# Sort stage of a graph kernel: one flag layout instead of two, and a strided read by TensorE

## The reference

```python
edge_index = jnp.stack([src, dst])
x = x + _L0_gnn_ref(_layernorm(x, axis=-1), edge_index, edge_weight, W, a1, a2)
x = x + _L0_ffn_ref(_layernorm(x, axis=-1)[None], ...)[0]
# inside the graph layer:
support = x @ W
r_D = jax.nn.sigmoid(support @ a2)
gated = r_D * support
msg = gated[col] * edge_values[:, None]
out = jax.ops.segment_sum(msg, row, num_segments=n)
sumnorm = jax.ops.segment_sum(edge_values * r_D[col, 0], row, num_segments=n)
```

## Time and profile before

| | |
|---|---|
| time before, median of 3 | 1416.52 us (1414.48 to 1417.66) |
| profiled execution, its own time | 1417.25 us |
| its span | 1415.4 us |
| granted TensorE clock, mean | 0.934 |
| busy: PE, DVE, POOL, ACT | 1187.8, 1079.2, 912.0, 371.0 us |
| POOL's gathers in the sort, after it | 294, 516 |

### The profile page before, as it was taken

How to read it: one execution, slowest core, us unless ns; L and a number is a source line. 1 busy time by engine, 2 the same in 40 slices (tenths; PEclk the granted TensorE clock), 3 DMA queues, 4 the chain that set the end, 5 groups by cost and what they waited for, 6 DMA issues and landing times.

```text
span 1415.4 us, 21674 instructions
## 1 busy us (share of the span) xinstructions
PE 1187.8 (84%) x6271; PEld 922.5 (65%) x6271; DVE 1079.2 (76%) x2744; ACT 371.0 (26%) x1224; POOL 912.0 (64%) x895
## 2 busy tenths in 40 slices
PE   3788588778988889798988898878888888887998
PEld 2677577767877778594556655555565555556887
DVE  8888999999999999537777677776776778764322
ACT  0334111111100100002333343333333334333232
POOL 0289677777777777757777777777777777760000
PEclk9889889999999999859999999999999999999999
DMA  8112345575545455725644445644444444431021
GB/s 271 34 60 72 54 112 150 148 158 152 146 134 138 136 145 140 156 64 125 135 119 126 118 126 124 131 122 125 118 126 120 126 121 123 125 105 35 34 78 70
DMA packets 163415, 166.39 MB, mean 118 GB/s; under 512 B 84677, under 2 KB 135897, under 8 KB 163308
## 3 DMA queue, kind: packets, MB, share of 16 engines
q0 software_dynamic: 39712, 108.02, 29.0%
q1 hardware_dynamic: 102428, 37.71, 11.2%
q10 hardware_dynamic: 21168, 19.35, 4.5%
HBM read 136.86 MB, written 28.14 MB: 117 GB/s over the span
## 4 chain that ended last, share of the span: by engine, by line
PE 33%; DVE 25%; POOL 17%; issue 13%; DMA 8%; POOLq 2%; ACT 1%; SPq 0%; DVEq 0%; ACTq 0%
PE bank L1700 32%; POOL rows L830 17%; DMA rows<-gated_rows_dram,ring_i 7%; DVE big L964 5%; DVE big L934 5%; DVE S L1113 3%; DVE big L918 2%; POOLq L822 2%; DVE big L949 2%; DVE big L925 2%; DVE big L942 1%; PE bank L1764 1%; DVE big L1050 0%; DMA big<-in_edge_weight_dram 0%; DVE bank L956 0%
## 5 line engine op out<-in xcount | busy, mean ns | idle before, releaser
L1700 PE MATMUL bank<-rows,S 128*128 128x257 f32 (+1 forms) x2254 | 603.1, 398 | 97.6 <-DMA rows<-gated_rows_dram,ring_i 76.0
L830 POOL DMA_INDIRECT rows<-gated_rows_dram,ring_i x516 | 511.0, 990 | 170.4 <-issue 146.5
L1700 PEld LDWEIGHTS bank<-rows,S 128*128 128x128 f32 x2254 | 408.1, 194 | 248.4 <-DMA rows<-gated_rows_dram,ring_i 140.7
L737 POOL DMA_INDIRECT rows<-gated_rows_dram,lg x294 | 290.7, 989 | 106.7 <-issue 73.3
L1700 PE MATMUL bank<-big 128*104 128x128 f32 (+3 forms) x1824 | 227.6, 288 | 71.3 <-DVE big L964 71.3
L1700 PEld LDWEIGHTS bank<-big 128*104 128x104 f32 (+2 forms) x1824 | 223.5, 194 | 80.7 <-issue 77.9
L1287 DVE TENSOR_SCALAR S<-iota,lof,srec 128x128 f32<-128x128 f32 x588 | 167.0, 358 | 1.5 <-PE bank L1700 1.4
L1298 DVE TENSOR_TENSOR ag<-bank,ovr 128x257 f32<-128x257 f32 x49 | 20.9, 427 | 153.2 <-PE bank L1700 153.0
L1544 ACT COPY ovr<-bank 128x257 f32<-128x257 f32 x98 | 36.8, 375 | 322.4 <-PE bank L1700 302.6
L1700 PE MATMUL bank<-Wxs,xT 128*128 128x512 f32 x196 | 112.0, 700 | 0.1
L1700 PE MATMUL bank<-xn,lg 128*128 128x256 f32 x392 | 102.0, 385 | 0.0
(11 more groups left out here) (260 smaller groups left out, 1410.5 us busy)
## 6 DMA issues: line engine op xcount, KB each, us to landing
overflow_sums_dram<-ovr ACTq DMA_DIRECT2D x98, 128.5 KB
rows<-gated_rows_dram,ring_i POOLq DMA_INDIRECT x516, 2.9
gated_rows_dram<-rows SPq DMA_DIRECT2D x49, 128.5 KB, 2.3
ovr<-overflow_sums_dram SPq DMA_DIRECT2D x49, 128.5 KB, 2.5
rows<-gated_rows_dram SPq DMA_DIRECT2D x49, 128.5 KB, 2.2
out_dram<-S SPq DMA_DIRECT2D x48, 128.0 KB, 1.7
rows<-gated_rows_dram,lg POOLq DMA_INDIRECT x294, 3.1
res<-in_x_dram SPq DMA_DIRECT2D x1, 4352.0 KB
```

Of the source, the lines that this page charges most:

```text
L737: pool.indirect_dma_start(rows[:, turn(n), :], None, gtab[:, :], bass.IndirectOffsetOnAxis(ap=ring1[:, n:n + 1], axis=0)).then_inc(s_row[t ...
L830: pool.indirect_dma_start(rows[:, slot(b, u), :], None, gtab[:, :], bass.IndirectOffsetOnAxis(ap=ring_i[:, b // CH % 2, n:n + 1], axis=0)) ...
L1700: return nc.tensor.matmul(o, l, r, start=start, stop=stop, skip_group_check=True)
```

## The change

The flags with columns innermost (`flags4`) and the step `mark` that makes them are gone. `lookup` now multiplies `flagsj`, with buckets innermost, so `prod` lies with buckets innermost as well. `quads` reads it across: its moving operand steps over 52 elements of two bytes from one column to the next, and is cut at whole buckets; the products of `later` are read as before.

```diff
-        flags4 = halved(carve(NX * HC, BF16), HC)
...
-            def mark(g):
-                step(v.tensor_tensor(flags4, hib[:, g * GC:(g + 1) * GC].rearrange("p (h j) -> p h j", h=2).unsqueeze(1)
-                                     .broadcast_to([P, NX, 2, HC]),
-                                     numbers(g).unsqueeze(2).unsqueeze(3).broadcast_to([P, NX, 2, HC]), ALU.is_equal))
...
             def lookup(g):
                 dve.wait_ge(s_base, 2 * g + 2)
-                v.tensor_tensor(halved(prod[:, 0:NX * GC], HC), flags4,
-                                bank[0][:, 0:4 * NX].rearrange("p (h v b) -> p h v b", h=2, v=2)[:, :, 0, :].rearrange("p h b -> p b h").unsqueeze(3).broadcast_to([P, NX, 2, HC]),
+                v.tensor_tensor(prod[:, 0:NX * GC].rearrange("p (h j b) -> p h j b", h=2, b=NX), flagsj[g % 2],
+                                bank[0][:, 0:4 * NX].rearrange("p (h v b) -> p h v b", h=2, v=2)[:, :, 0:1, :].broadcast_to([P, 2, HC, NX]),
                                 ALU.mult).then_inc(s_prod, 1)
...
-            mark(0)
             lookup(0)
-            dve.wait_ge(s_prod, 1)
-            mark(1)
             centre()
...
-                if g + 1 < NG:
-                    mark(g + 1)
...
                 o = quad_at(g)
                 wide = o.shape[-1]
-                for n in range(0, (NX + HC) * GC, wide):
+                across = prod[:, 0:NX * GC].rearrange("p (j b) -> p b j", b=NX)
+                for b in range(0, NX, wide // GC):
+                    n = min(wide // GC, NX - b)
+                    mm(o[:, 0:n * GC], identb, across[:, b:b + n, :], b == 0, False)
+                for n in range(NX * GC, (NX + HC) * GC, wide):
                     w = min(wide, (NX + HC) * GC - n)
-                    m = mm(o[:, 0:w], identb, prod[:, n:n + w], n == 0, n + wide >= (NX + HC) * GC)
+                    m = mm(o[:, 0:w], identb, prod[:, n:n + w], False, n + wide >= (NX + HC) * GC)
```

## The result

The kernel after took 1425.01 us (median of 6 runs, 1422.31 to 1429.25), the kernel before 1416.33 us beside it: 8.7 us slower, ratio 1.0072 with a 95% interval of 1.0054 to 1.0090. The prediction was 1408, faster. The profiled execution after took 1424.05 us, its span 1422.2.

A forecast was written before the change was run, and what follows sets the result against it. The prediction took POOL's gather issues to bound the sort, DVE being nearly as full. Its terms, -1.9 - 1.9 - 8.1 + 2.8 = -9.1 us, gave 1408 us, range 1402 to 1424.

The forecast's parts named there:

- this middle one: PE's read across in `quads`: 0.92 ns a column, from one fp32 instruction, against 0.51 contiguous; +0.7 us a group.
- The lower end: PE's read across in `quads`: the step costs nothing, 0 us a group, from DVE's stepped sum over PSUM.
- free: Rival: PE's read across in `quads` costs nothing (k = 1); -11.9 us, 1405; chance 0.22.
- the upper end: PE's read across in `quads`: 1.85 ns a column, +2.2 us a group; chance of slower 0.20.
- Rounds 1 to 4: PE and ACT set the pace, so a longer `quads` shifts all: 4 x 0.7 = +2.8 us (ends 0 and +8.9).
- Rounds 5 to 25: PE's loop of 17.1 us grows to 17.8, just POOL's 17.83 a round; cost taken as 0.
- Together +9, 1425: Rival, read at upper end: early rounds +5.1, later PE loop 19.3 gives +3.5; up to 1435; chance of slower 0.20.
- the rest of the span: From the sort's last gather on, it hangs on POOL's gathers and moves as a whole; last 830 us unchanged.
- `mark(0)`: Before `lookup(0)`, which PE's next work waits for: removing it takes its 1.88 us off the path, -1.9 us.
- `mark(5)`: Round 4, ahead of the decoding that POOL's first gather waits for: removing it gives -1.9 us.
- The 8.1 us of POOL's idle time: Late rounds, POOL's waits after 418 us: all that POOL lets through of 37.6 us removed from DVE, -8.1 us.
- `quads` takes over 2.5 us: Sign that the prediction is wrong; `quads` was expected at 1.8 us instead of 1.11, 3.3 at the upper end.

The follow-up runs named there:

- e1: Kernel after, but DVE's lookup reads the flags across in all groups and PE reads contiguously; 1408.68 us, ratio to before 0.9957.
- f1: Kernel after, but PE reads the products in runs of 12 (early rounds) or 8 neighbouring buckets per column; 1401.43 us, ratio to before 0.9898.
- f2: f1 with the removed flags written again, unread, for groups 6 to 25; 1417.06 us, ratio to before 1.001.
- e4: Kernel before with groups of 17 bf16 products at various steps and runs appended at its end; 4.11 us for 17 at 104 bytes, 0.95 at 2 bytes.

## Why the prediction was wrong

- **The price of PE's read, the step that failed.** The prediction took "this middle one", +0.7 us a group, with ends of 0 and +2.2. Measured: 3.55 - 1.11 = +2.4, 1.89 ns a column instead of 0.92. The row that was nearest in value was the upper bound (1.85 ns a column), not the fp32 instruction at 0.92; both rows had been chosen for what they show of data rate, and neither has a step in SBUF. The lower end came from DVE's sum over PSUM; in SBUF DVE pays for a step as well (0.87 ns an element, e1). The only statement about steps in SBUF, the rule on 16-byte lines, was set aside for want of a size. It ruled out "free", which got 0.22, and stood nearer to the upper end.
- **Rounds 1 to 4.** The mechanism was right: a longer `quads` shifts them, and without `mark` DVE's wait at 118.44 us grew as forecast (2.46 us at 119.86, for 0.33 before; 2.2 expected). The size was 4 x the price; it was 4.0 + 3.5 in two rounds, of which 1.3 in round 2 is the lower clock behind the read, and 0 in round 4, whose `quads` had 2.7 us to spare.
- **Rounds 5 to 25.** The rival that the prediction kept for the upper end is what happened: "Together +9, 1425", with PE's loop at 19.3. The loop is 19.5 to 20.1, in two rounds 21.6, and POOL's waits grew by 9.8 instead of 3.5; the early rounds gave +3.0 at the first gather instead of +5.1. That the rival hit 1425 is luck in part: it had one error up and one down, the sends got 2.8 us shorter, and the rest of the span gave 3.5 back, against the claim that it moves as a whole. The forecast itself took 0 here, from a loop of 17.8 us; with the measured price that step falls too.
- **`lookup`, and what `mark` was worth.** 1.88 us was right. `mark(0)` brought 2.5 us for the 1.9 expected (`quad` of round 1 at 80.87 for 83.41), `mark(5)` 1.9: from `quad` to the first gather 12.19 us for 14.12. The 8.1 us of POOL's idle time were real, and f1 wins nearly all of them.
- **What bounds the kernel.** POOL's issues are the floor, as said: f1 ends at them, with sends 17.7 to 18.5 us apart in the later rounds, and no kernel is below 17.7. But more went with `mark` than the waits show: 2.8 us stood inside a few long sends, which the prediction took for POOL's own work. That and the longer `quad` of f2 are most of why f2 pays 15.6 and not 8.1 for its 37.6 us.
- **The check list.** "`quads` takes over 2.5 us" and "the early rounds" of 24 us were the right things to look at; the first line of the groups decides the case.

## What to carry to other kernels

A transposed layout moves a cost, and what it comes to depends on who pays. For the same products it was +1.4 us a group as DVE's read, +2.4 as TensorE's read and +5.6 as DVE's write. For TensorE bf16 columns 16 or more bytes apart take four times as long, while a step of 4 bytes or runs of 16 contiguous bytes are free. So cut the operand such that an instruction takes 8 neighbours from each row (f1: 1401.4 us, the fastest kernel here), and the layout that suits VectorE costs TensorE nothing. When no row shows the access, put the forecast at the upper bound or measure it alone first, and read the granted clock beside every such measurement. Before giving time away on an engine with "slack", add up its loop with the hand-overs: PE had 17.1 of 19.05 us in use, and 2.4 more made it the bound.

## What was not expected of the hardware

- TensorE's granted clock fell to 0.50 behind 3.7 us of reading across that left PE busy all along, in rounds 2 and 3, where it stays at 1.00 with the read in runs. In e4 it fell too while PE read with a step and was busy all along: 1.00 at 8 bytes, a mean of 0.91 at 16, 0.50 at 24.
- TensorE's price for a column by itself, about 1.8 ns, was the same at a granted clock of 0.50 as at 0.91 and 1.00.
- VectorE's stepped write is dearer than its stepped read: 7.46 us at 64 bytes against 3.32 at 104, and 1.88 contiguous.
- One of POOL's scatters took 3.48 us beside a VectorE operation that touches none of its data, and 1.79 where that operation was removed. The mean of the 26 (1170 and 1061 ns) hides that nearly all take 1.02.
